# Second layer: the attention output is turned by four small DMA transposes per tile, in place of TensorE's last block of transposes

## The reference

```
x = x + L0_xattn(layernorm(x), ctx)     # 32 heads of 128, 8 key/value groups
x = x + L0_ffn(layernorm(x))            # relu^2 MLP, latent expert, layernorm
x = x + L1_xattn(layernorm(x), ctx)     # 32 heads of 16, 8 key/value groups
x = x + L1_ffn(layernorm(x))            # 8 experts, the two highest logits are averaged

# L1_xattn, as used here
q = rmsnorm(h) @ wq.T ; k = ctx @ wk.T ; v = ctx @ wv.T     # k, v repeated 4 times
o = softmax(q k.T / 4) v                                     # per sequence and head
y = o.reshape(tokens, 512) @ wo.T
```

## Time and profile before

| | us |
|---|---|
| median of three runs | 1778.09 (1776.77 to 1781.56) |
| the profiled execution, its own time | 1777.49 |
| span of the profile, first to last instruction | 1775.7 |
| PE busy | 1689.4 (95%) |
| DVE busy | 1209.6 (68%) |
| ACT busy | 716.1 (40%) |
| POOL busy | 485.0 (27%) |

### The profile page before, as it was taken

The page is one execution under the profiler, slowest core; times in us unless marked ns, Lnnn a source line. Parts: engine busy times, 40 slices in busy tenths (PEclk is TensorE's granted clock), DMA queues, the critical chain, the costliest instruction groups (busy, mean ns, idle before and its releaser), DMA issues. The chain is left out here.

```text
span 1775.7 us, 31943 instructions
## 1 busy us (share of the span) xinstructions
PE 1689.4 (95%) x12512; PEld 889.1 (50%) x12512; DVE 1209.6 (68%) x2304; ACT 716.1 (40%) x1295; POOL 485.0 (27%) x371
## 2 busy tenths in 40 slices
PE   5889999999999999999999999998999999999998
PEld 2444555555555555555455544444444545455443
DVE  5776666665656565656566577777888888888873
ACT  5443433333333333333333423234455555445442
POOL 0143570702605308028300000000023333233334
PEclk9899999999999999999999999999999999999999
DMA  6122151411412304114421230011453554544340
GB/s 243 36 60 72 49 178 13 143 48 27 164 25 81 110 14 143 49 47 156 131 73 25 68 93 9 16 24 48 155 107 72 92 87 84 93 81 95 71 86 18
DMA packets 231213, 141.52 MB, mean 80 GB/s; under 512 B 215072, under 2 KB 215328, under 8 KB 223136
## 3 DMA queue, kind: packets, MB, share of 16 engines
q1 hardware_dynamic: 163488, 122.77, 25.2%
q10 hardware_dynamic: 67584, 16.79, 5.4%
HBM read 65.60 MB, written 20.97 MB: 49 GB/s over the span
## 5 line engine op out<-in xcount | busy, mean ns | idle before, releaser
L774 PE MATMUL bank<-R 128*128 128x512 f16 (+1 forms) x7152 | 1294.9, 341 | 23.9 <-DVE R L1664 8.6
L774 PEld LDWEIGHTS bank<-R 128*128 128x128 f16 x7152 | 585.0, 98 | 671.6 <-issue 32.0
L1664 DVE SCALAR_TENSOR_TENSOR R<-bank,biases,R 128x512 f16<-128x512 f32 x288 | 204.4, 746 | 221.3 <-ACT R L1242 178.6
L629 POOL TENSOR_TENSOR R<-R 128x512 f32<-128x512 f32 x112 | 144.7, 1292 | 319.8 <-ACT R L1450 317.4
L1242 ACT ACTIVATE R<-bank,biases 128x512 f16<-128x512 f32 x128 | 87.6, 686 | 258.8 <-PE bank L774 249.4
L516 POOL TENSOR_SCALAR R<-R 128x2048 f32<-128x2048 f32 (+1 forms) x20 | 33.1, 1654 | 415.6 <-PE bank L774 351.3
L1450 ACT ACTIVATE R<-R,msk 128x512 f32<-128x512 f32 x128 | 90.0, 718 | 113.5 <-DVE R L2015 113.3
L774 PE MATMUL bank<-CT,R 128*128 128x512 f16 x384 | 95.0, 400 | 22.8 <-DVE CT L1638 11.5
L1676 DVE SCALAR_TENSOR_TENSOR R<-bank,R 64x512 f16<-64x512 f32 x64 | 44.0, 688 | 98.8 <-ACT R L1250 98.4
L1749 DVE SCALAR_TENSOR_TENSOR X<-bank,X 128x512 f32<-128x512 f32 x128 | 86.7, 683 | 32.3 <-PE bank L774 32.1
L2015 DVE SCALAR_TENSOR_TENSOR R<-bank,R 128x512 f32<-128x512 f32 x128 | 85.2, 678 | 28.2 <-PE bank L774 27.5
(11 more groups left out here) (161 smaller groups left out, 1624.6 us busy)
## 6 DMA issues: line engine op xcount, KB each, us to landing
R<-in_wB SPq DMA_DIRECT2D x16, 1024.0 KB, 5.9
R<-in_wX SPq DMA_DIRECT2D x16, 1024.0 KB, 4.8
w_split<-AW SPq DMA_DIRECT2D x16, 1024.0 KB, 4.8
R<-w_split SPq DMA_DIRECT2D x12, 1024.0 KB, 7.0
R<-in_ctxT SPq DMA_DIRECT2D x4, 1024.0 KB, 10.0
X<-in_x SPq DMA_DIRECT2D x4, 1024.0 KB, 13.9
out<-X SPq DMA_DIRECT2D x16, 256.0 KB, 2.0
R<-in_wB SPq DMA_DIRECT2D x7, 512.0 KB, 5.6
```

Of the source, the lines that this page charges most:

```text
L629: g.tensor_tensor(acc, acc, tmp[:, e % 2, :], ALU.add).then_inc(e_acc, 1)
L774: last = pe.matmul(dst, a(sa), b(sb_), start=(k == 0), stop=(k == m - 1))
L1664: v.scalar_tensor_tensor(out=dst, in0=src, scalar=bias, in1=hi, op0=ALU.add, op1=ALU.subtract).then_inc(done, 1)
```

## The change

For tiles 2 to 15 `turn_o` on TensorE and `turned_o` on ScalarE are gone. SyncE issues four DMA transposes of 64x512 instead, two per sequence (one for each 64 rows of `onh`), behind the turning of the keys of tile n+1 and ahead of `turn_attn(n + 2)`. They wait for the low half of their sequence and for the output product of the tile before (`a_y`), which frees `oT`. `output` waits for all four (`o_in`) and for the gate's bank to be read (`r_lg`), a wait that stood ahead of `turn_o`. From tile 3 on ScalarE waits, before it writes `onh`, for the four of the tile before. Tiles 0 and 1 stay as they were.

```diff
+            def turn_o(n, b):
+                sp.wait_ge(b_olo, n * 2 + b + 1)
+                sp.wait_ge(a_y, n)
+                for u in range(2):
+                    sp.dma_start_transpose(REST.oT[:, :, u, 64 * b:64 * b + 64],
+                                           REST.onh[64 * u:64 * u + 64, b].rearrange("p s n -> p (s n)")).then_inc(o_in, 16)
 ...
                 if n < NT - 1:
                     turn_q(n + 1)
                     turn_k(n + 1)
+                turn_o(n, 0)
+                turn_o(n, 1)
                 if n < NT - 2:
                     turn_attn(n + 2)
 ...
             def output(n):
-                pe.wait_ge(a_toev, n + 1)
+                if n < 2:
+                    pe.wait_ge(a_toev, n + 1)
+                else:
+                    pe.wait_ge(o_in, (n - 1) * 64)
+                    pe.wait_ge(r_lg, n)
 ...
                 weigh_v(n, 1)
                 expert(n - 1, 3, this)
-                pe.wait_ge(r_lg, n)
-                turn_o(n)
                 expert(n - 1, 4, this)
 ...
             def out_hi(n, b):
                 act.wait_ge(b_on, n * 2 + b + 1)
+                if n >= 3:
+                    act.wait_ge(o_in, (n - 2) * 64)
 ...
                 out_hi(n, 1)
-                turned_o(n)
```

More of the change, by code:

```diff
@@ L261, in build @@
         fn_in, an_in = sem("fn_in"), sem("an_in")
+        o_in = sem("o_in")
         q_in, k_in, pr_in = [sem("q_in0"), sem("q_in1")], sem("k_in"), sem("pr_in")
```

## The result

The changed kernel took 1839.8 us as a median, the kernel before 1779.8 in the same comparison: a ratio of 1.0341 (1.0317 to 1.0364), 60 us slower. (One of the four executions of the kernel before took 5328 us; it is not in the ratio.) The direction and the place were forecast, the size was not: the forecast was 1793, the range ended at 1817.

The account below looks back on a forecast made before the run. TensorE's list was taken to bound the kernel. Waits of 1.6 us less 0.44 saved, 15.1 us over thirteen steps, less 0.4 in step 15, gave +14.7 us on the 1778.1 median: 1793 us, range 1777 to 1817.

Parts of the forecast that it names:

- the bound (TensorE's list): TensorE, busy 367.8 of 370.9 us in the touched stretch, sets the 30.9 us period; added waits count in full.
- the saving's place: Eight transposes gone from TensorE's path save 0.44 us a tile, 6.2 us in fourteen tiles; ScalarE's copies count nothing.
- the room of 3.16 us: Time on SyncE from the keys' issue end to the output product, 3.6 us less the 0.44 saved.
- the wait ahead of the output product: TensorE waits 1.6 us for the four transposes in steps 2 to 14: chain 4.75 us, 3.16 there.
- it comes again in each step: SyncE's chain start moves with TensorE, so nothing gives the wait back; net 1.16 us a step, 15.1 for thirteen.
- the price of an issue: SyncE's hold for each small transpose behind the first: taken as 0.6 us, with ends of 0.33 and 1.23.
- the clock: Rival: waits halve TensorE's clock; none expected at 1.6 us, 11 us more atop the fixed price; within that rival's 0.32.
- The line through packets: SyncE's issue time taken to grow with packets: 256 packets take 0.70 us, or about 0.46 drawn from the store.
- The hold of 1.3 for the first issue: On SyncE, the first new issue lasts until the keys' transfer is through, 1.3 us; zero as other end.
- the landing: The last 64 KB transpose lands 2.05 us after its issue, between 2.0 and 3.3 us.
- The rival with a fixed price: Each transpose's issue holds SyncE 1.23 us whatever its size; wait 2.85 us, 1802 to 1822 us; chance 0.32.
- fewer and larger transfers: On SyncE, two transposes over 128 rows in place of four: a wait of 0.3 us in place of 1.6.

Follow-up runs that it names:

- e1: The kernel before plus the four small DMA transposes per tile into unused columns, nothing of TensorE waiting for them; 1780.1 us, ratio 0.9997.
- e7: The changed kernel without any turning of the attention output in tiles 2 to 15, its result being another; 1773.7 us, ratio 0.9967.
- e10: The changed kernel with 6 matmuls of 128x512 in each wait ahead of the output product; 1819.9 us, ratio 1.0221.
- e6: The changed kernel with each tile's output product one expert later on TensorE, behind expert 5 of the next step; 1820.6 us, ratio 1.0229.
- e11: The kernel before plus four small DMA transposes per tile into unused columns, the output product waiting for them; 1822.7 us, ratio 1.0261.
- e9: The changed kernel with sequence 0's two transposes issued between queries and keys, sequence 1's behind the keys; 1843.4 us, ratio 1.0357.
- e5: The changed kernel with 12 matmuls of 128x512 in each wait ahead of the output product; 1827.9 us, ratio 1.0259.

## Why the prediction was wrong

Right were the bound (TensorE's list), the saving's place, the room of 3.16 us (3.2 measured), the wait ahead of the output product and of nothing else in steps 2 to 14, and that it comes again in each step. `turn_attn` and ScalarE's wait cost nothing (e1). Two steps failed: the price of an issue and the clock.

*The price of an issue.* "I take 0.6": it was 1.24. The line through packets was drawn between a plain store and the medians of two transposes, and one of these, the 1.94 us of 128x2048, was no price of an issue: its row has 1.32 as its least. The lone transposes of 128x1024 lie at 1.23, and that was the nearest row. The hold of 1.3 for the first issue wasn't there as such (1.20 right behind the keys), and the landing took 2.35 in place of 2.05. So from the keys' issue the chain has 0.1 of gap, then 3.8 for three issues with their gaps, then 2.35, 6.3 us in place of 4.75. Less 3.2 that is 3.1 us of wait in a plain step, 3.3 as a mean. The rival with a fixed price had 2.85 for this.

*The clock.* It was put down as a rival worth 11 us, in half of the waits, and only on top of the other one. The clock fell after 12 of 13 waits, and five of the twelve stretches lasted twice the 3.4 us that it had been priced by. What the clock cost is read from TensorE's busy time: 441.6 us in the stretch, against 414.4 in e7, which has as many matmuls there. e7's rows:

```profile
1323.90:1747.50 423.60, 414.36 (x3282) 206.55 (x3280) 343.55 (x805) 198.78 (x429) 141.77 (x111) 1.00 0.46 84
```

The sum, from the stretch of 428.3 us before:

| | us |
|---|---|
| transposes gone, as e7 shows it | -4.7 |
| waits ahead of the output product | +42.8 |
| the same matmuls with the clock at one half | +27.2 |
| other waits | +0.7 |
| changed kernel's stretch | 494.3 |

Two other readings agree with the third term: e10 had some 22 us of it back by keeping TensorE at work, with one stretch at 0.50 left, and at 0.50 for 61 us of the stretch no more than 30.7 can be lost. The forecast's 14.7 us had 6.2 us for the first term, 20.8 for the second, which is half of it, and nothing for the third. The two errors may go together: single waits of 1.6 to 1.8 us had the full clock behind them in e6 and e11. But two of 1.78 and 1.05 us had not (e9), and no run has the forecast's wait by itself.

The prediction's fewer and larger transfers, two of 128 rows in place of four, weren't run. With the prices measured here the chain would be 0.1 + 1.2 + 0.05 and a landing between 2.35 (64 KB) and 3.2 us (256 KB). I estimate a wait of 0.5 to 1.4 us from that, still no gain.

The Trainium skill's advice on TensorE ("TensorE: Matmul & The Clock Gate", section "Why this matters for your kernels"), to leave no idle gaps between bursts, is borne out by e5, e10 and e11: the mean granted clock of the stretch is 0.94 with the gaps, 0.97 with e11's shorter ones and 1.00 with fillers in them. I had given it a small chance where the trace already showed it in two waits of three.

None of these versions that turn the attention output beats the kernel before. e7 leaves that work out altogether and gains 0.3%.

## What to carry to other kernels

Before you move work from a busy engine to a DMA queue, add up the whole chain on that queue, and give each DMA transpose the price of the instruction (here 1.24 us of the issuing engine, and 2.3 us to the landing), however little it moves: four of 64 KB hold SyncE for 5.07 us, one of 256 KB for 1.23. Count what a wait does to TensorE's clock as a term of its own; here it added 64% to the waits. And where a wait has to stay, look whether the thing behind it is on a chain to another engine, before you shift it.

## What the runs showed that I had not expected

A DMA transpose of 16 KB, 64 KB or 256 KB holds SyncE for the same time, 1.22 to 1.24 us; the landing grows only from 2.3 us (16 and 64 KB) to 3.2 us (256 KB).

The clock's fall can't be told from the longest wait alone. A wait of 3.15 us in the changed kernel had the full clock behind it:

```profile
1550.51 2.76 PE L784 MATMUL bank<-AW,R 128*128 128x512 f16 x12 [3.15 <-DMA R<-R]
```

while one of 2.13 us in the same kernel had half of it:

```profile
1371.03 4.45 PE L784 MATMUL bank<-AW,R 128*128 128x512 f16 x12 [2.13 <-DMA R<-R]
...
1371.20:1374.60 3.40, 3.40 (x9) 1.21 (x8) 0.70 (x2) 2.16 (x4) 0.38 (x1) 0.50 0.42 81
```

Waits of 3.3 us as a mean brought a half clock in 12 of 13 steps; of 2.65 us (e11) in 7; of 1.8 us with six matmuls ahead (e10) in one. What decides the single case these runs don't show.

Transposes of 64 KB now and then land after 3.0 to 4.4 us in place of 2.3, beside a 16 KB packet of instruction loading. In e5 such a packet met one of the four in each step, in e10 in one of 13.
